# Matmuls of zeros where the plan expects TensorE to wait, in a two-layer transformer kernel planned by a cost model

## The reference, cut to what matters

```python
mod = (_silu(L0_c) @ L0_wmod).reshape(8, 6, 1, -1)
sa, ca, ga, sb, cb, gb = (mod[:, n] for n in range(6))
h = _layernorm(x) * (1 + ca) + sa
x = x + ga * _L0_attn_ref(h, ...)     # causal softmax(q k^T + alibi) v, projected
h = _layernorm(x) * (1 + cb) + sb
x = x + gb * _L0_ffn_ref(h, ...)      # gate, key, square, value with a token shift
# the second layer: attention with rotary embedding, then one linear map (W plus a low-rank part)
```

## Time and profile before

| | us |
|---|---|
| median of 3 runs | 2815.2 |
| lowest, highest | 2811.31, 2816.49 |
| the profiled execution | 2814.14 |
| its span, first to last instruction | 2812.1 |
| PE busy | 2448.3 |
| DVE busy | 2278.1 |
| mean granted clock of PE | 0.951 |

### The profile page before, as it was taken

The page is one execution under the profiler, slowest core; times in us unless marked ns, Lnnn a source line. Parts: engine busy times, 40 slices in busy tenths (PEclk is TensorE's granted clock), DMA queues, the critical chain, the costliest instruction groups (busy, mean ns, idle before and its releaser), DMA issues.

```text
span 2812.1 us, 54982 instructions
## 1 busy us (share of the span) xinstructions
PE 2448.3 (87%) x18968; PEld 1041.3 (37%) x18968; DVE 2278.1 (81%) x7158; ACT 1711.8 (61%) x3458; POOL 850.1 (30%) x954
## 2 busy tenths in 40 slices
PE   6798877988989898988989989998989889887586
PEld 4223434323334333343434333443333434333223
DVE  4899747899987998978988898878989788962872
ACT  3286563676765576665766656755766657665164
POOL 3211351234222432225232342224322252225121
PEclk8799988999999999999999999999999999998789
DMA  7511125113312222322322123222232223001200
GB/s 232 149 47 31 37 72 146 53 35 98 118 49 83 78 79 91 90 69 76 106 68 80 57 90 100 77 77 73 76 93 89 69 80 104 22 30 61 86 19 16
DMA packets 142393, 218.28 MB, mean 78 GB/s; under 512 B 21190, under 2 KB 62556, under 8 KB 142052
## 3 DMA queue, kind: packets, MB, share of 16 engines
q1 hardware_dynamic: 142120, 214.77, 24.7%
HBM read 137.87 MB, written 77.89 MB: 77 GB/s over the span
## 4 chain that ended last, share of the span: by engine, by line
PE 55%; DVE 31%; ACT 7%; issue 4%; POOL 2%; DMA 1%; SPq 0%; DVEq 0%; ACTq 0%; POOLq 0%
PE ctx_ps L1627 12%; PE big L1608 11%; PE big L1545 11%; DVE small L1371 10%; PE small L1586 8%; PE big L1534 8%; DVE mx L1369 6%; PE big L1659 4%; ACT probs L1146 4%; ACT xn L1195 2%; DVE region L1439 2%; DVE stats L1314 2%; PE big L1642 2%; DVE mx L1371 2%; DVE region L1477 1%
## 5 line engine op out<-in xcount | busy, mean ns | idle before, releaser
L1146 ACT ACTIVATE probs<-big 128x512 f32<-128x512 f32 (+2 forms) x2560 | 1221.2, 563 | 509.2 <-PE big L1608 500.2
L1371 DVE CUSTOM_DVE_ANT_0 small<-small,mask 128x128 f32<-128x128 f32 (+3 forms) x2048 | 941.3, 518 | 158.2 <-PE small L1586 151.8
L1608 PE MATMUL big<-stack_q,stack_k 64*128 64x512 f16 (+3 forms) x6144 | 709.2, 331 | 65.5 <-ACT probs L1146 40.5
L1056 POOL TENSOR_SCALAR_AFFINE_SELECT probs<-probs 128x512 f32<-128x512 f32 x512 | 329.5, 653 | 1347.3 <-ACT probs L1146 1347.0
L1369 DVE TENSOR_REDUCE mx<-small 128x1 f32<-128x512 f32 x1024 | 652.3, 681 | 53.3 <-PE small L1586 45.9
L1627 PE MATMUL ctx_ps<-probs,v_ones 128*17 128x512 f32 (+3 forms) x6144 | 634.8, 501 | 8.5 <-POOL probs L1056 7.6
L1586 PE MATMUL small<-stack_k,stack_q 64*128 64x512 f16 (+3 forms) x3072 | 466.2, 341 | 195.0 <-DVE mx L1371 110.6
L1608 PEld LDWEIGHTS big<-stack_q,stack_k 64*128 64x128 f16 x6144 | 250.4, 95 | 491.9 <-issue 297.7
L1586 PEld LDWEIGHTS small<-stack_k,stack_q 64*128 64x128 f16 x3072 | 122.1, 94 | 693.2 <-DVE mx L1371 347.1
L1371 DVE DVE_READ_ACCUMULATOR2_ANT mx<- 128x1 f32 x2048 | 283.8, 139 | 0.0
L1534 PE MATMUL big<-hT,w_qkv 128*128 128x512 f32 x512 | 259.6, 623 | 0.3 <-issue 0.2
(11 more groups left out here) (93 smaller groups left out, 1913.3 us busy)
## 6 DMA issues: line engine op xcount, KB each, us to landing
image<-region SPq DMA_DIRECT2D x192, 256.0 KB
stack_q<-image SPq DMA_DIRECT2D x64, 512.0 KB, 3.7
stack_k<-image SPq DMA_DIRECT2D x64, 512.0 KB, 4.6
lo_dram<-region SPq DMA_DIRECT2D x64, 256.0 KB
w_qkv<-wqkv SPq DMA_DIRECT2D x16, 768.0 KB, 5.1
x_res<-x SPq DMA_DIRECT2D x32, 256.0 KB, 3.2
stack_q<-lo_dram SPq DMA_DIRECT2D x128, 64.0 KB, 3.9
stack_k<-lo_dram SPq DMA_DIRECT2D x128, 64.0 KB, 4.6
```

The lines of the kernel that those rows point to most:

```text
L1056: g.affine_select(out=diag, in_=diag, compare_op=ALU.is_ge, fill=0.0, base=0, pattern=[[0, GH], [1, P]], channel_multiplier=-1).then_inc(m ...
L1146: s.activation(probs[:, n % HELD, heads, q0:], big[:, at.slot(turn), 0:len(pairs) * width] .rearrange("p (h q) -> p h q", h=len(pairs)), A ...
L1371: last = v.tensor_tensor_reduce(out=held, in0=held, in1=mask[:, BANK - width:], scale=1.0, scalar=3.0 * NEG, op0=ALU.add, op1=ALU.max, acc ...
L1608: last = te.matmul(big[:, at.slot(at.turn() + parity), j * width:(j + 1) * width], stack_k[rows, c, g * PAIR_N + pair, kt * P:(kt + 1) * P ...
```

## The change

`Model` now keeps the stretches in which PE works (`worked`). Before an item is played, `plan` asks `model.warm(model.needs(item))`: when the model expects PE to wait at least 500 ns for it, the next bank of `big` is free, and PE has by the model worked no more than 0.6 of the time just before the wait's end, an item `warm` is put ahead of it, with as many zero matmuls as fit into the expected wait less 150 ns, at 165 ns each. On PE a `warm` item waits for that bank and then multiplies zeros of `mask` by zeros of `mask` into it, 384 columns of bf16 each, with as many rows and columns as the items around it use. Whatever is written there is overwritten by the bank's next user. No other engine does anything for it.

```diff
+WARM_WAIT, WARM_BUSY = 500.0000, 0.6000
+WARM_NS, WINDOW = 165.0, 3413.0
...
+    def warm(self, until):
+
+        wait = until - self.free["PE"]
+        if wait < WARM_WAIT or self.ring[self.turn % RING] > self.free["PE"] or self.busy(until) > WARM_BUSY:
+            return 0
+        n = int((wait - 150) / WARM_NS)
+        self.worked.append((self.free["PE"], self.free["PE"] + n * WARM_NS))
+        self.free["PE"] += n * WARM_NS
+        return n
...
+        idle = model.warm(model.needs(item))
+        if idle:
+            out.append(("warm", item[1], idle, model.shape or 128))
         model.play(item)
...
-                if kind == "mods":
+                if kind == "warm":
+
+                    wait_bank(pe, at)
+                    rows, cols = slice(0, 64 if item[3] == 64 else P), slice(0, 32 if item[3] == 32 else P)
+                    for _ in range(item[2]):
+                        te.matmul(big[cols, at.slot(), 0:BANK - P], mask[rows, cols], mask[rows, 0:BANK - P],
+                                  start=True, stop=True)
+                elif kind == "mods":
```

More of the change, by code:

```diff
@@ L228, in __init__, with busy @@
         self.ready, self.pipe = {}, 0.0
+        self.worked = []
+    def busy(self, now):
+        while self.worked and self.worked[0][1] < now - WINDOW:
+            self.worked.pop(0)
+        return sum(min(b, now) - max(a, now - WINDOW) for a, b in self.worked if a < now) / WINDOW
     def at(self, *keys):
@@ L335, in play, with take @@
     def play(self, item):
+        self.take(item)
+        self.worked.append((self.began, self.free["PE"]))
+    def warm(self, until):
[6 more added lines that the diff above has]
+        return n
+    def take(self, item):
         kind, unit = item[0], item[1]
         begin = max(self.free["PE"], self.needs(item))
+        self.began = begin
         shape = self.shape_of(item)
```

## The result

The change makes the kernel slightly slower. Taken together on one chip, the changed kernel takes 2820.3 us (median of 11 executions, 2816.4 to 2828.3) and the kernel before 2812.8 (11, 2810.9 to 2819.5). The ratio is 1.0025, 95% interval [1.0014, 1.0036]. By the medians that is +7.5 us, where +7.9 was forecast. The profiled execution took 2817.4 us, 3.3 more than the one of before.

The account below looks back on a forecast made before the run. PE and DVE were taken to bound the kernel in turn, PE's clock falling after idling. Costs of 30.9 us less 23.0 given back made +7.9 us on the 2815.2 median: 2823, range 2810 to 2838.

Parts of the forecast that it names:

- 52 before qk(1): Block before qk(1), where PE waits only 0.12 us: costs 9.3 us, with some 6 zero matmuls at half clock.
- warming up: Max-stream steps where the clock has already fallen: four steps with five zero matmuls each 0.6 us longer, 2.4 us lost.
- steps of both long stretches: Twelve max-stream steps on the chain per long stretch go from 1.43 to 1.21 us: 4.8 us back.
- score behind the first: Score after the first long stretch, 1.73 us, would take 0.86 at full clock: 0.9 us back.
- its transposes: Sixteen transposes ahead of qk(1), 3.67 us against 1.76 at full clock; half the gain taken: 0.9 us back.
- first modulations: First modulations, 6.98 us against 4.12 for the same 32 later; a third of the gain taken: 0.9 us back.
- last y: Last y, 5.81 us for sixteen matmuls against 3.46; 0.7 of 2.3 us taken back, the clock being down already.
- short stretches: Six short stretches preceded by zero matmuls, 27.07 us of PE work at half clock: 8 us back, at most 13.5.
- 1 (everything comes back, 2812): Every clock fall with zero matmuls ahead is averted and warming up costs nothing: -3 us, 2812; chance 0.22.
- 2 (half of each slow stretch returns, 2780): Half of the 122.9 us at half clock with zero matmuls in or ahead returns: 2780 us; chance 0.05.
- 3 (half the rows don't hold the clock): Half-row zero matmuls don't hold the clock up; long-stretch steps 0.6 us longer, nothing comes back: 2885 or more; chance 0.06.
- 4 (the big blocks at half clock): Blocks of 52, 33 and 63 run partly at half clock after idling: about 15 us more, 2838; chance 0.10.

Follow-up runs that it names:

- second and third kernel of experiment 2: Kernel before with only 247 zero matmuls between max-stream steps: all on 128 rows, 2801.4 us (0.9976); only the block of 21 on 128 rows, 2806.6 us (0.9981).
- experiment 2: Kernel before with only the 247 zero matmuls between max-stream steps; the one meant here has them on 64 rows: 2819.0 us, 1.0038.
- experiments 5 and 4: Changed kernel with counts from traced waits plus 58 new places, 64 rows: 2774.1 us, 0.9878; changed kernel without the 52 before qk(1): 2809.8 us, 1.0006.

## Why the prediction was right

The sign and the mechanism were right: five blocks of zero matmuls where PE has nothing to wait for, a clock that stays up in both long stretches, and a small remainder. That the remainder came out within half a us of the measured one is partly luck: two errors of 7 to 10 us, shown below, nearly cancel in the sum. Term by term, from the shifts in the trace (us):

| term | forecast | trace |
|---|---|---|
| 52 before qk(1) | 9.3 | 8.6 |
| 18 before the first max | 2.9 | 2.9 |
| 7 before qk(0) | 1.1 | 1.1 |
| 33 before qk(3) | 5.1 | 4.9 |
| 63 before max(15) | 6.3 | 6.3 |
| 21 and 9 near the end | 0.8, 1.9 | 0.7, 1.2 |
| warming up | 2.4 | 1.7, at another place |
| steps of both long stretches | -4.8 | -2.8, -1.9 |
| score behind the first | -0.9 | -0.2 |
| transposes and more behind the second | -1.4 | -1.7 |
| qk(1) | -1.3 | -1.2 |
| its transposes | -0.9 | 0 |
| transposes at 421 | -1.8 | -1.6 |
| gates at 485 | -2.3 | -2.1 |
| first modulations | -0.9 | 0 |
| last y | -0.7 | -2.1 |

**The price of one.** 0.162 us at full clock in every block, as forecast (0.161), and 0.32 at half. The estimate of 0.115 us from the Trainium skill (TensorE: Matmul & The Clock Gate, Back-to-back issue gap, its figures for a sustained stream) does not fit; that section's columns over the clock plus 2.5 ns, 0.1625 us, does. The 52 took 9.14 us: the first few at half clock, the rest at full.

**The steps.** 1.21 us from 126.52 to 127.73 in the first stretch, as forecast. In the second 1.27, which is DVE's doing: between its reductions it also takes small steps of a layer norm. From the timeline of the changed kernel, DVE:

```profile
2626.83 0.15 DVE L1363 TENSOR_TENSOR tmp<-rstd 128x8 f32<-128x8 f32 x1
2626.90 1.28 DVE L1396 TENSOR_REDUCE mx<-small 128x1 f32<-128x512 f32 x2
2628.10 0.15 DVE L1365 TENSOR_TENSOR tmp<-tmp,ve 128x8 f32<-128x8 f32 x1
2628.18 1.28 DVE L1396 TENSOR_REDUCE mx<-small 128x1 f32<-128x512 f32 x2
```

From one pair of reductions to the next are 1.28 us, so PE at full clock has only 1.28 and not 1.21 to fall to, and the second stretch gives back 1.9 instead of 2.4.

**Its own misses.** The 22 ahead of turned(1) did not save the transposes: 4.33 us without work were left behind them, and the transposes ran at half (the first of the stretches shown above), 3.68 us as in the earlier trace rows. Likewise 3.35 us between the 13 and the modulations, which took 6.97 us as before. I had taken a part of each (0.9 and 0.9) as a compromise between all and nothing; it was nothing both times. The score behind the first stretch gave back 0.2 instead of 0.9: DVE, not PE, ends the steps around it. At the last y I took 0.7 for fear that the clock was down there already; timeline of PE, changed kernel:

```profile
2805.54 2.56 PE L1600 MATMUL big<-mask 128*128 128x384 bf16 x9
2807.93 3.62 PE L1572 MATMUL big<-w_ffn,hT 128*128 128x256 f32 x16
```

The nine run mostly at half (0.28 us each) and the y behind them runs at full, 3.62 us against 5.81. The short stretches were forecast at 8. Three of them can be read: the projection near 104 (-1.4), the fall at 459 that did not come (-1.4), and at 2674.30 the clock fell all the same, and three steps with eight, five and five zero matmuls cost 1.7 us up to the score behind them.

**What the sum did not have.** Between 550 and 2400 us the change has zero matmuls at two places only (five at 786.8, at half clock, +0.67; fourteen at 2393, the last six at half clock, +0.6 where I had nothing), and yet the shift goes from 4.5 behind the first of them to 0.0 ahead of the second: the clock falls at other moments than in the profiled execution of before. Another -2.75 lies between 218 and 302 us, and -1.5 between 29 and 56, of which 1.1 is lost again by 67. Such drift is not due to zero matmuls nearby: between 735 and 2540 us it lay between 0 and -11 us in the nine kernels with none or nearly none there. It goes with the time at half clock between 560 and 2400 us: in the second and third kernel of experiment 2 (-0.5 and -0.1 us) that was 92.2 and 95.6 us, against 95.6 before; in the change (-3.2) it was 88.7, in the other six (-6.7 to -10.8) 61.4 to 71.7. What decides in a given kernel whether these falls come is not shown. Added up, the places with zero matmuls cost some 29 us and gave back 16, and the drift took 10 of the remaining 12 to 13; that is the profiled execution's +3. The forecast had 30.9 and 23.0. It met the median's +7.5, but it had the return too high by 7 us near the zero matmuls and no drift at all, and the two nearly cancel: that is the luck in it. How much of the drift is in the medians too, these runs don't tell.

**The rivals.** *1 (everything comes back, 2812)* is refuted for the change, whose interval lies above 1; it is what the change becomes with 128 rows (1.0005) or without the 52 (1.0006). *2 (half of each slow stretch returns, 2780)* is refuted. It came from the Trainium skill (TensorE: Matmul & The Clock Gate, HAM oscillation), throttled time times one half. Here 99.4 us fewer at half clock would be an estimated 50 us by that rule, and the trace does not agree: the places with zero matmuls gave back 16 and the drift 10. In the kernel without the overrunning blocks 124 us fewer were worth 14 us by the ratio and 22 by the spans of the profiled executions: 0.11 to 0.18 of the throttled time, since DVE sets the pace in most of it. *3 (half the rows don't hold the clock)* was half right, and I had it at 0.06. Its mechanism exists in another form: in the changed kernel the clock stayed up under them; where it was down, the stretch stayed down with them and each step was 0.6 us longer, 9.8, 9.9 and 15.0 us in the three traces that show it. *4 (the big blocks at half clock)* happened only to the 7 in the kernel with blocks alone (0.32 us each) and to the first four or five of the 52.

**The step that was wrong in itself** is "Warming up": "four such steps: 4 x 0.6 = 2.4", which assumes that a step with five zero matmuls brings the clock back. With 64 rows it did not within the 45 us of steps in experiment 2, nor in the 33 and 34 us of those in experiments 5 and 4. In the changed kernel this stayed hidden: the block of 63, on all rows, stands ahead of the second stretch, and the first began at full clock. The overrunning block is thus not pure loss, but 22 on all rows, in the wait of 3.88 us, did the same for nothing. The kernel without the overrunning blocks, timeline and stretch:

```profile
2585.60 3.74 PE L1624 MATMUL big<-mask 128*128 128x384 bf16 x22
2589.99 0.39 PE L1644 MATMUL small<-stack_k,stack_q 64*128 64x128 f16 x4 [0.66 <-DMA stack_k<-lo_dram]
```

```profile
2590.00:2625.00 35.00, 31.82 (x208) 14.91 (x209) 34.46 (x141) 5.08 (x10) 2.34 (x2) 1.00 0.35 97
```

## What to carry to other kernels

Work that only keeps the clock up is worth having where the engine really waits; take its amount from a trace and not from the planner's expected wait, since on the critical path each unit beyond the real wait goes straight into the end (here the difference between 1.0025 and 0.9950). Use all rows of the array for it: the price is the same 0.16 us, and it decided here whether a fallen clock comes back. Look for places the model does not see (here 58 short waits worth about 20 us), and put such a block of all rows where a stretch begins, because with half the rows these stretches went on at the clock they began with.

## What the hardware showed that I had not expected

- With matmuls of zeros on 64 of 128 rows between the steps, the clock was at full through both long stretches of the changed kernel (steps of 25 and 27 us), but at half for 54.61, 40.96 and 40.96 us in three others, in which PE was busy for 51.7 of 54.6 us and for 40 of 41. In these three it came back only behind the steps, 5 to 6 us after work on all rows (transposes, or scores two at a time) had begun. On 128 rows the clock rose within the block of 21 that stands there. Whether the rows count or something that goes with them, such as the max matmuls that no longer start together, was not taken apart.
- Matmuls whose operands are all zero are enough for the clock: it rose at 2609.11 inside the block of 21, with nothing else on PE. No run compares them with other data.
- The same instructions, same place: in the kernel without the 52 the clock was at full before the steps of the first long stretch (PE busy for 3.86 of 4.78 us just before) and fell at 109.78, while the changed kernel with the same instructions there did not fall. Two of twelve executions of one kernel seem to have gone the costly way. I cannot say what decides it.
